# Causal mask of the self-attention maxima: from a matrix product to a fused add-and-max on VectorE

## The reference, cut to what matters

```
scores = (gt * scores_cross + (1.0 - gt) * scores_conv) * scale
causal = jnp.tril(jnp.ones((s, s), dtype=bool))
scores = jnp.where(causal[None, None], scores, -jnp.inf)
attn = jax.nn.softmax(scores, axis=-1)
out = jnp.einsum('bhqk,bkhd->bqhd', attn, V).reshape(b, s, H * hd)
```

## Time and profile before

| | us |
|---|---|
| median of 3 runs | 1063.05 |
| the profiled execution, its own time | 1057.54 |
| its span, first to last instruction | 1055.8 |
| TensorE busy | 1015.4 |
| VectorE busy | 721.9 |
| ScalarE busy | 577.1 |

### The profile page before, as it was taken

How to read it: one execution, slowest core, us unless ns; L and a number is a source line. 1 busy time by engine, 2 the same in 40 slices (tenths; PEclk the granted TensorE clock), 3 DMA queues, 4 the chain that set the end, 5 groups by cost and what they waited for, 6 DMA issues and landing times.

```text
span 1055.8 us, 19123 instructions
## 1 busy us (share of the span) xinstructions
PE 1015.4 (96%) x7108; PEld 599.0 (57%) x7108; DVE 721.9 (68%) x1603; ACT 577.1 (55%) x1093; POOL 198.9 (19%) x220
## 2 busy tenths in 40 slices
PE   4999899999999999999999999999999999999998
PEld 3877344444444444444444466444544688888887
DVE  7778887878787878887777376765666454555552
ACT  3776276767666766676767567576557311111110
POOL 6655000000000000000000024211010133333331
PEclk9999799999999999999999999999999999999999
DMA  8596904444433444444320047788753100000001
GB/s 262 196 270 222 194 2 82 83 82 83 73 59 55 72 80 83 87 86 75 60 43 12 9 100 187 182 160 141 126 101 71 23 28 2 20 21 20 20 21 40
DMA packets 82186, 93.27 MB, mean 88 GB/s; under 512 B 14660, under 2 KB 75296, under 8 KB 80557
## 3 DMA queue, kind: packets, MB, share of 16 engines
q1 hardware_dynamic: 79511, 88.85, 38.6%
q10 hardware_dynamic: 2582, 3.20, 1.4%
HBM read 53.55 MB, written 28.80 MB: 78 GB/s over the span
## 4 chain that ended last, share of the span: by engine, by line
PE 76%; DVE 15%; ACT 3%; issue 3%; DMA 2%; SPq 1%; POOL 0%; POOLq 0%; DVEq 0%; ACTq 0%
PE bank L134 19%; PE bank L837 12%; PE bank L870 11%; PE bank L856 9%; DVE pm L767 7%; PE bank L1539 3%; PE bank L860 3%; PE bank L842 2%; PE bank L1438 2%; PE bank L1141 2%; PE bank L968 2%; PE bank L1428 2%; PE bank L1430 2%; PE bank L1411 2%; PE bank L1413 1%
## 5 line engine op out<-in xcount | busy, mean ns | idle before, releaser
L767 DVE TENSOR_REDUCE pm<-bank 128x1 f32<-128x512 f32 (+3 forms) x608 | 356.8, 655 | 86.3 <-PE bank L842 69.6
L814 ACT ACTIVATE prob<-bank 128x512 f32<-128x512 f32 (+1 forms) x608 | 317.4, 583 | 171.8 <-PE bank L860 86.5
L837 PE MATMUL bank<-stk,stq 96*128 96x512 bf16 (+3 forms) x768 | 223.7, 335 | 5.3 <-DVE pm L767 3.2
L856 PE MATMUL bank<-stq,stk 98*128 98x512 bf16 (+3 forms) x768 | 220.7, 327 | 1.7 <-DMA stq<-mrow 0.8
L837 PEld LDWEIGHTS bank<-stk,stq 96*128 96x128 bf16 x768 | 67.9, 97 | 134.4 <-DVE pm L767 77.1
L870 PE MATMUL bank<-prob,va 128*17 128x512 f32 (+3 forms) x1536 | 143.8, 492 | 0.0
L1666 ACT ACTIVATE e_sg<-bank 128x512 f32<-128x512 f32 x48 | 28.7, 598 | 176.7 <-PE bank L134 174.6
L1378 ACT ACTIVATE xprob<-bank 80x512 f32<-80x512 f32 x128 | 72.7, 594 | 60.9 <-PE bank L1430 56.9
L753 POOL TENSOR_TENSOR xres<-xres,bo_b 128x256 f32<-128x256 f32 x32 | 23.2, 726 | 398.4 <-DVE pm L767 204.2
L856 PEld LDWEIGHTS bank<-stq,stk 98*128 98x128 bf16 x768 | 69.1, 98 | 45.4 <-ACT prob L814 9.1
L842 PE MATMUL bank<-tri_q,identb 128*128 128x128 bf16 (+2 forms) x352 | 87.0, 247 | 0.0
(11 more groups left out here) (183 smaller groups left out, 1334.3 us busy)
## 6 DMA issues: line engine op xcount, KB each, us to landing
qk<-a_parts SPq DMA_DIRECT2D x32, 384.0 KB, 2.8
xq<-c_parts SPq DMA_DIRECT2D x16, 384.0 KB, 2.7
xstq<-xq SPq DMA_DIRECT2D x32, 192.0 KB, 4.2
stq<-qk SPq DMA_DIRECT2D x30, 192.0 KB, 3.9
stk<-qk SPq DMA_DIRECT2D x15, 384.0 KB, 6.4
vs<-a_vst SPq DMA_DIRECT2D x8, 544.0 KB, 3.8
oall<-u_out SPq DMA_DIRECT2D x64, 64.0 KB
xstq<-xq SPq DMA_DIRECT2D x32, 128.0 KB, 4.6
```

What stands on the lines that cost most here:

```text
L767: nc.vector.tensor_reduce(pm[:, k, h0:h0 + hb, r], src[:, 0:hb * w].rearrange("p (h w) -> p h w", h=hb), AX, ALU.max).then_inc(s_mxe, 1)
L814: nc.scalar.activation(prob[:, U % NPS, 0:hb * n], bank[STB[U % NSB]][:, 0:hb * n], ACT.Exp).then_inc(s_ex, 1)
L837: mm = nc.tensor.matmul(dst[:, h * w:(h + 1) * w], stq[i][0:R, half, h0 + h, r * P:(r + 1) * P], stk[i][0:R, h0 + h, k0:k0 + w], start=(h ...
L856: mm = nc.tensor.matmul(dst[:, h * n:(h + 1) * n], stk[i][0:RM, h0 + h, kt * P:(kt + 1) * P], stq[i][0:RM, half, h0 + h, q0:q0 + n], start ...
```

## The change

The product L842 goes, and `tri_q` with it. A new constant `past` of 128 x 512 bf16 holds zeros in its first 384 columns and the triangle in its last 128. For a unit at the diagonal VectorE now takes one `tensor_tensor_reduce` for each head: it adds the last w columns of `past` to the head's w columns in the bank, writes the sums back into the same columns, and writes their maximum into `pm`. The semaphore `s_mxe` is raised by the last one of a unit. The 16 full units are reduced as before.

```diff
-        tri_q = sb(root, "tri_q", [P, HG, P], BF16)
+        past = sb(root, "past", [P, 512], BF16)
...
+            nc.gpsimd.memset(past[:, 0:512 - P], 0.0).then_inc(s_con, 1)
...
-                nc.gpsimd.tensor_copy(tri_q[:, h, :], trif[:, 0, :]).then_inc(s_con, 1)
...
+            nc.gpsimd.tensor_copy(past[:, 512 - P:512], trif[:, 0, :]).then_inc(s_con, 1)
...
-                half, k, r, h0, hb, _, w, _ = mx_units[m]
-                nc.vector.tensor_reduce(pm[:, k, h0:h0 + hb, r],
-                                        src[:, 0:hb * w].rearrange("p (h w) -> p h w", h=hb),
-                                        AX, ALU.max).then_inc(s_mxe, 1)
+                half, k, r, h0, hb, _, w, diag = mx_units[m]
+                if diag:
+                    for h in range(hb):
+                        s = src[:, h * w:(h + 1) * w]
+                        last = nc.vector.tensor_tensor_reduce(s, s, past[:, 512 - w:512], 1.0, NEG, ALU.add, ALU.max,
+                                                              pm[:, k, h0 + h:h0 + h + 1, r])
+                    last.then_inc(s_mxe, 1)
+                else:
+                    nc.vector.tensor_reduce(pm[:, k, h0:h0 + hb, r],
+                                            src[:, 0:hb * w].rearrange("p (h w) -> p h w", h=hb),
+                                            AX, ALU.max).then_inc(s_mxe, 1)
...
-                                          start=(h == 0), stop=not diag, skip_group_check=True)
-                if diag:
-                    mm = nc.tensor.matmul(dst[:, 0:hb * w].rearrange("p (h w) -> p h w", h=hb)[:, :, w - P:w],
-                                          identb[:], tri_q[:, 0:hb], start=False, stop=True, skip_group_check=True)
+                                          start=(h == 0), stop=True, skip_group_check=True)
```

More of the change, by code:

```diff
@@ L338, in qkv_gpsimd @@
                                         channel_multiplier=1).then_inc(s_con, 1)
-                g.wait_ge(s_con, 8 + part)
+                g.wait_ge(s_con, 9 + part)
             power1(g, 1)
             for h in range(HG):
-                nc.gpsimd.tensor_copy(tri_q[:, h, :], trif[:, 0, :]).then_inc(s_con, 1)
                 nc.gpsimd.tensor_copy(tri_k[:, h, :], trif[:, 1, :]).then_inc(s_con, 1)
                 nc.gpsimd.tensor_scalar(negid[:, h, :], ident[0:MR, 0:SK], NEG, None, ALU.mult).then_inc(s_con, 1)
+            nc.gpsimd.tensor_copy(past[:, 512 - P:512], trif[:, 0, :]).then_inc(s_con, 1)
             nc.gpsimd.tensor_copy(identb[:], ident[:]).then_inc(s_con, 1)
             nc.gpsimd.tensor_copy(sel[:], self_[:]).then_inc(s_con, 1)
-            g.wait_ge(s_con, 10 + 3 * HG + 2)
+            g.wait_ge(s_con, 11 + 2 * HG + 3)
             g.wait_ge(s_kl, 2)
```

## The result

The changed kernel took 1082.73 us (median of 4 runs, 1080.44 to 1084.87) against 1062.55 for the kernel before (4 runs): ratio 1.0174, 95% interval 1.0131 to 1.0216. It is slower by about 20 us; the quotient of the two medians is 1.0190, inside the interval. A second series of six runs gave 1.0173 (1.0144 to 1.0202). Its profiled execution took 1083.7 us, with a span of 1082.0.

The account below looks back on a forecast made before the run. VectorE was taken to pace most self-attention stretches, though TensorE counts as busy. Groups 29.7 us plus group 0's 1.6 and 0.8 gave 32.1; 1057.5 + 32.1 = 1089.6, 1095 with 5.5 added. Range 1064 to 1168; own case 1078 to 1120.

Parts of the forecast that it names:

- Rival C: Self-attention groups: TensorE's path sets the end and VectorE's idle time absorbs its new work; faster, 1037 us; chance 0.07.
- seven to nine units without a pause: VectorE in a group: it reduces that many units, then idles once, six times a group, 6.30 us idle in sum.
- the idle pieces: VectorE's six pauses in a group: they shrink from 6.30 to 5.12 us, absorbing 1.18 of 3.16 us new work.
- f: Fixed VectorE cost of one head's fused call, both instructions together: taken as 0.14 us, bounds 0.06 and 0.31.
- the 0.08 for the second instruction: VectorE's instruction writing one column of `pm`: starts 0.08 us after the main one, like tiny independent instructions.
- rival D: VectorE's in-place sum, read from and written to the same bank, goes at half rate: 1270 us or so; chance 0.05.
- A: VectorE's second instruction waits for the first, f = 0.31: group + 6.4 us, median 1165 us; chance 0.17.
- B: VectorE's second instruction is nearly free, f = 0.08: about 7 us in all, 1070 us; chance 0.08.
- the 29.7 us for the groups: The 15 groups with maxima made beside another group's scores: each grows by 1.98 us.
- The burst: Group 0's stretch of 23 VectorE units without a pause: 16 heads in 11 units cost 1.6 us in full.
- The units among the projections: Group 0's 11 other units: the same cost as in the burst, half hidden by guess, 0.8 us.
- the 5.5 us by which I raised the forecast: Whole kernel: the profiled execution was 5.5 us below the median of the runs, so 1089.6 became 1095.

Follow-up runs that it names:

- e2: Changed kernel with the mask product L842 kept beside the sum on VectorE: 1092.2 us, 1.0247 of the kernel before.
- e1: Kernel before without the mask product of the maxima, so it does not compute the layer: 1049.7 us, 0.9852 of the kernel before.
- e6: Changed kernel with the sums written to a bf16 scratch tile in SBUF instead of back into the bank: 1066.4 us, 1.0015 of the kernel before.
- e5: Changed kernel with all 38 units fused, full units adding a tile of zeros: 1088.9 us, 1.0228 of the kernel before.
- e4: Changed kernel fused only in units of four and two heads, one-head units keeping their mask product: 1080.8 us, 1.0140 of the kernel before.
- e10: Changed kernel with the reciprocals of the softmax sums moved to in front of unit 21 of the next group: 1077.7 us, 1.0132 of the kernel before.
- e3: Changed kernel fused only in one-head units (384 and 512 keys), the others keeping mask product and one reduction: 1063.6 us, 0.9992 of the kernel before.

## Why the prediction was right in kind, and where its sum was off

**Who paces.** VectorE and the three banks do, in most stretches: VectorE's new work alone costs 1.60 us a group (e2), and 1.76 us of TensorE's work were worth 0.97 or 0.71, never all (e1, e2). Rival C falls. What I wrote of seven to nine units without a pause, six times a group, was too even: between the idle pieces stand 8, 9, 2, none, 7 and 12 units. The sum used the units as they stand.

**The cost of a head.** I took f = 0.14, between 0.06 and 0.31; it is 0.115, and 0.07 for the first call of a row. Of the 0.14, the 0.08 for the second instruction was the wrong part. It costs no time in the queue that could be told apart: its read starts with the next call. By the Trainium skill, VectorE: DVE Perf Modes, section "Two Vector instructions with no wait between them", nothing here is held. The trace agrees, with starts 0.65 apart for calls that last 0.73. What I gave the second instruction belongs to two other things. About 0.015 is what the fused form costs in SBUF over a reduction (e6's 0.075 against 0.06). Another 0.04 comes with the sums written into the bank, which I had priced at nothing or, in rival D, at half the rate; it is a small fixed cost. Rivals A and D fall, each by its spacing. B's price of 0.08 is not that of the changed kernel, but its picture of the second instruction was the right one: e6 has 0.075. That 0.14 came near 0.115 is in part luck.

**The idle pieces.** Forecast 1.32, 1.10, 0.96, 0.13, 1.09 and 0.52, in sum 5.12; measured 1.29, 1.10, 0.98, 0.12, 1.14 and 0.40, in sum 5.03. Each held to about a tenth. At the measured f = 0.115 the same steps give 5.25, so this came out 0.2 too long.

**The sum.** At f = 0.115 the same steps give a group 1.33 longer, not 1.98. Measured were 0.90. VectorE's work grew by 2.17 (0.90 + 6.30 - 5.03) where 32 x 0.115 - 1.32 is 2.36; with 8 of the 32 calls at 0.07 it would be 2.0. The idle fell by 1.27. So of the 29.7 us for the groups, 13.5 came, and 1.5 more beside the reciprocals. The mis-sized term is f first, 15 x 0.65 or about 10 us of the difference; the cheaper first calls and the idle pieces share the rest. The burst cost 1.1 instead of 1.6, which is what f = 0.115 gives (16 x 0.115 - 0.66 = 1.2). The units among the projections cost 0 instead of 0.8, so VectorE has room there.

**The term that I did not have.** The profiles differ by 26.2 us, of which 13.5 + 1.5 + 1.1 = 16.1 are explained so. Nearly all of the rest is TensorE's clock: 4.4 us behind the reciprocals and 4.9 behind the last group. The 0.9 that are left are the first group's (32.51 us instead of 30.67), which in the changed kernel starts at half clock and stays there until 131 us; they are not parted further. In the kernel before, the profiled execution was at half clock only in the burst (mean 0.994); thirteen timed runs of it in one later series stood between 0.973 and 0.990. So the 5.5 us by which I raised the forecast were probably such stretches, though no trace of a timed run shows where. The changed kernel's profile (0.980) has some already (613 and 743 us). From median to median the change is 20.2 us: 16.1 by the burst and by the groups at full clock, and 4.1 left, for which the 4.4 us of half clock inside self-attention account in size. Without them the time would have been near 1078, the lower edge of my own range. That it lies clearly inside is luck: it is owed to a term that I did not have.

That TensorE's waits bring these stretches on is borne out by the waits behind the reciprocals, read in all profiles. With 0.86, 0.40 and 0.20 us in a row the clock fell in six of nine cases (the changed kernel twice, e5), with 0.74 and 0.40 in two of three (e4). With 0.82 and 0.22 (e6), with 0.53 and 0.28 (e2), with one wait of 1.06 (e1) and with less in the other kernels it never fell. With the reciprocals moved (e10), one wait of 0.20 is left and the clock held. In e2 VectorE is as loaded as in the changed kernel and only TensorE's waits are shorter, which speaks against the load of VectorE as the cause. It is one profile each, two of the changed kernel, and the same waits were followed by a drop in one execution and not in another; what else decides is open.

## What to carry to other kernels

An engine that is 96% busy can still be the one that waits: look at where its third buffer comes free, then count the work in front of that point and the work behind it apart. Count the calls when you fuse two operations: where a unit stayed one call the group got 0.19 us shorter (e3), where one reduction became two or four calls it got 0.95 longer (e4), though as many mask columns were saved. Fuse unit by unit where the loaded engine idles anyway, and let a throw-away result go to a bf16 tile in SBUF rather than back into the bank it came from (e6).

## What the hardware showed that I had not expected

- A fused add and maximum with its sums written in place into a PSUM bank starts every 0.65 us for 512 columns and 0.25 for 128, behind another one; into a bf16 tile in SBUF, 0.61 and 0.21. The first call of a row is followed after 0.61 and 0.20 to 0.22 in either. The read of the accumulator lasts 0.14 in the one and 0.08 in the other.
- TensorE fell to half its clock behind a row of waits of 0.86, 0.40 and 0.20 us, and stayed there for about 7 us (315.9 to 322.7 us), although it was at work again; the other seven such stretches behind the reciprocals lasted about 3.4 us. Such stretches also come in stages that no edit touched (613, 743 us), in some executions and not in others.
